# A decoder layer's expert stage: earlier statistics, a later weight request, token numbers from one accumulation

## The reference

```
x = x + self_attention(layernorm(x))                     # 16 heads, causal
x = x + cross_attention(layernorm(x), context, mask)     # 16 heads
x = x + experts(layernorm(x))

def experts(x):                       # x: 4096 tokens x 512
    probs = softmax(x @ Wg + bg)      # 8 experts
    a = argmax(probs)                 # one expert a token
    h = gelu(x @ W1[a] + b1[a])       # 512 -> 512
    y = h @ W2[a] + b2[a]             # 512 -> 512
    return probs[a] * y
```

## Time and profile before

| | us |
|---|---|
| median of 3 runs | 2126.4 (2125.07 to 2128.78) |
| the profiled execution | 2124.88 |
| its span, first to last instruction | 2123.1 |
| start of the expert stage | 1740.8 |
| first gather starts | 1810.8 |
| first tile's rows normalized from | 1820.7 |
| first tile's W1 matmuls from | 1825.0 |

### The profile page before, as it was taken

One profiled execution on the slowest core, in us unless ns is written; L12 is line 12 of the kernel. 1 busy time (PEld: TensorE's weight loads), 2 busy tenths in 40 slices (PEclk: granted clock), 3 DMA queues, 4 the chain that ended last, 5 costly groups with the idle time before them and its releaser, 6 DMA issues. The chain is left out here.

```text
span 2123.1 us, 34283 instructions
## 1 busy us (share of the span) xinstructions
PE 1914.8 (90%) x10910; PEld 1328.5 (63%) x10910; DVE 1384.7 (65%) x2824; ACT 1140.5 (54%) x2168; POOL 1006.4 (47%) x1030
## 2 busy tenths in 40 slices
PE   4899999999999856999999999999999965799997
PEld 3666666767676634556666666666566424698896
DVE  4666666666666625667767676767676527588886
ACT  3555555555555423555555555555555425587785
POOL 2446565564655652444444444344444326345544
PEclk9999999999999977999999999999999867799999
DMA  5334444444434334333434343434333239322220
GB/s 157 89 93 113 121 131 108 127 105 125 135 98 118 101 107 137 83 89 79 115 81 120 80 120 76 124 72 106 94 100 76 61 94 378 109 95 70 88 88 25
DMA packets 133301, 227.47 MB, mean 107 GB/s; under 512 B 30522, under 2 KB 31586, under 8 KB 133152
## 3 DMA queue, kind: packets, MB, share of 16 engines
q1 hardware_dynamic: 109920, 194.93, 33.2%
q0 software_dynamic: 12704, 29.51, 5.1%
q10 hardware_dynamic: 10528, 1.17, 0.4%
HBM read 94.92 MB, written 37.31 MB: 62 GB/s over the span
## 5 line engine op out<-in xcount | busy, mean ns | idle before, releaser
L391 POOL TENSOR_TENSOR cross_probs<-cross_probs 128x1024 f32<-128x1024 f32 x128 | 304.7, 2384 | 361.8 <-ACT cross_probs L493 361.1
L591 DVE TENSOR_REDUCE cross_m_col<-cross_sS 128x1 f32<-128x512 f32 x512 | 340.1, 686 | 186.4 <-PE cross_sS L744 182.7
L493 ACT ACTIVATE cross_probs<-cross_sT 128x512 f32<-128x512 f32 x512 | 305.5, 599 | 271.0 <-PE cross_sT L760 266.5
L594 DVE CUSTOM_DVE_ANT_0 self_sS<-self_sS,self_tri 128x128 f32<-128x128 f32 (+3 forms) x512 | 248.8, 503 | 184.5 <-PE self_sS L744 181.3
L493 ACT ACTIVATE self_probs<-self_sT 128x256 f32<-128x256 f32 (+3 forms) x512 | 222.7, 439 | 241.8 <-PE self_sT L760 238.9
L379 POOL TENSOR_SCALAR_AFFINE_SELECT self_probs<-self_probs 128x256 f32<-128x256 f32 x256 | 106.8, 423 | 324.0 <-ACT self_probs L493 324.0
L744 PE MATMUL cross_sS<-cross_stack 97*128 97x512 f32 x512 | 210.8, 420 | 29.1 <-DVE cross_m_col L591 19.0
L760 PE MATMUL cross_sT<-cross_stack 98*128 98x512 f32 x512 | 214.9, 433 | 2.2 <-ACT cross_probs L493 2.2
L391 POOL TENSOR_TENSOR self_probs<-self_probs 128x512 f32<-128x512 f32 (+1 forms) x128 | 210.9, 1668 | 0.3 <-ACT self_probs L493 0.3
L760 PE MATMUL self_sT<-self_stack 98*128 98x256 f32 (+2 forms) x512 | 176.1, 357 | 2.4 <-ACT self_probs L493 2.4
L760 PEld LDWEIGHTS cross_sT<-cross_stack 98*128 98x128 f32 x512 | 95.5, 192 | 130.4 <-ACT cross_probs L493 79.1
(11 more groups left out here) (244 smaller groups left out, 4600.1 us busy)
## 6 DMA issues: line engine op xcount, KB each, us to landing
self_stack<-self_stage SPq DMA_DIRECT2D x384, 128.0 KB, 2.4
cross_stack<-cross_stage SPq DMA_DIRECT2D x288, 128.0 KB
self_rows<-in_x_dram SPq DMA_DIRECT2D x64, 256.0 KB, 3.6
moe_w<-in_L_ffn_W_dram SPq DMA_DIRECT2D x16, 1024.0 KB, 14.8
cross_stack<-cross_stage POOLq DMA_DIRECT2D x96, 128.0 KB, 3.3
x_after_self<-self_rows SPq DMA_DIRECT2D x32, 256.0 KB, 2.4
x_after_self_and_bias<-self_ahead SPq DMA_DIRECT2D x32, 256.0 KB, 2.3
cross_rows<-x_after_self SPq DMA_DIRECT2D x32, 256.0 KB, 4.3
```

The source lines that it names most:

```text
L391: pool.tensor_tensor(total, total, tile_of(n, kb)[:, js, q0:S], ALU.add).then_inc(added, 1)
L493: act.activation(tile_of(n, kb)[:, j, q0:S], sT[:, i % 2, q0:S], ACT.Exp, scale=SCALE).then_inc(exp_done, 1)
L591: dve.tensor_reduce(to, sS[:, k % 2], AX_X, ALU.max).then_inc(s_free, 1)
L594: dve.tensor_tensor_reduce(sS[:, k % 2, 0:width], sS[:, k % 2, 0:width], tri[:, S - P - qb * P:S - P - qb * P + width], 1.0, LOWEST, ALU.a ...
```

## The change

- VectorE's and TensorE's waits for the constants move: VectorE's behind the statistics of batch 4, TensorE's (with b1's transpose) behind the first two turned tiles. ScalarE's copy of b1 goes behind the third turned tile.
- SyncE requests b2 for the first three tiles, then waits until the first tile's rows have been gathered, and only then requests expert 3's weights.
- The tile numbers carry 128 x tile - 8192 from the start (`iota`). So the products for partition and tile can be summed in one PSUM accumulation: 64 matmuls of 52 columns in place of 32 of 104. One VectorE step, done once for `cur` (6 columns) and once for `ids` (52), takes the place of three; the first three tiles' `cur` needs no copy on GpSimd.
- `weigh` of pairs 0 to 2 moves ahead of the last `choose`; the exponentials of pairs 0 to 2 move ahead of the last `take_gate`. Of the four stores only two stand ahead of ScalarE's part of `at_col`, the other two behind it. Gelu's table is loaded behind the stores.

```diff
-            for e in [e for e in range(E) if e != LENT] + [LENT]:
-                if e < NB:
+            for e in range(E):
+                if e < LENT:
                     sp.wait_ge(loaded[weight_sem[e]], 16)
-                if e == LENT:
-                    sp.wait_ge(placed, 4)
-                load_weights(e)
+                if e != LENT:
+                    load_weights(e)
             sp.wait_ge(experts_ready, 1)
...
+            for i in range(RING):
+                tile(0, i)
+            sp.wait_ge(placed, 4)
+            sp.wait_ge(loaded[weight_sem[LENT]], 16)
+            sp.wait_ge(gathered[0], 16 * R)
+            load_weights(LENT)
+            with sp.Fori(1, LAPS) as lap:
...
-            for n, step, base, of_p in ((NT, 1, -NO_ROW // P, 0), (1, 1, 0, 1), (LEVELS, TOK, 0, 0),
+            for n, step, base, of_p in ((NT, P, -NO_ROW, 0), (1, 1, 0, 1), (LEVELS, TOK, 0, 0),
...
+            def gather(t, i, copied=True):
+                if copied:
+                    pool.tensor_copy(cur[:, i], ids[:, bass.ds(t * R, R)]).then_inc(cur_ready, 1)
...
             for t in range(RING):
-                gather(t, t)
+                gather(t, t, copied=False)
+            pool.wait_ge(ids_ready, 2)
...
             normalize_batch(0)
-            act.wait_ge(const_step, 12)
-            act.wait_ge(g_full, 1)
-            act.copy(b1_cols[:].rearrange("p e k -> p (e k)"), b1_bank)
...
                 take_turned(b, 2)
+                if b == 0:
+                    act.copy(b1_cols[:].rearrange("p e k -> p (e k)"), b1_bank)
                 take_turned(b, 3)
+            for i in range(PAIRS - 1):
+                exponent(i)
             take_gate(B - 1)
-            for i in range(PAIRS):
-                exponent(i)
-            act.preload_act_table(ACT.Gelu)
-            for i in range(PAIRS):
+            exponent(PAIRS - 1)
+            for i in range(2):
                 store_rec(i)
...
                 act.activation(at_col[:, ts, 0], same_col[:, ts], ACT.Copy, scale=numbers_p).then_inc(col_ready[0], 1)
+            for i in range(2, PAIRS):
+                store_rec(i)
+            act.preload_act_table(ACT.Gelu)
...
-            dve.wait_ge(const_loaded, 16 * 3)
             for b in range(B):
                 row_stats(b)
+                if b == 4:
+                    dve.wait_ge(const_loaded, 16 * 3)
...
-            for i in range(2, PAIRS):
-                choose(i)
-                if i == 2:
-                    spread_counts(0)
+            choose(2)
+            spread_counts(0)
+            for i in range(PAIRS - 1):
+                weigh(i)
+            choose(PAIRS - 1)
             spread_counts(1)
-            for i in range(PAIRS):
-                weigh(i)
+            weigh(PAIRS - 1)
...
             dve.wait_ge(placed, 4)
-            step(dve.tensor_scalar(id_f, sorted_[:, 1], float(P), None, ALU.mult))
-            stepped()
-            step(dve.tensor_tensor(id_f, id_f, sorted_[:, 0], ALU.add))
-            stepped()
-            dve.tensor_scalar(ids[:], id_f, float(NO_ROW), None, ALU.add).then_inc(ids_ready, 1)
+            for to in (cur[:].rearrange("p i r -> p (i r)"), ids[:]):
+                n = to.shape[1]
+                dve.tensor_scalar(to, sorted_[:, 0:n], float(NO_ROW), None, ALU.add).then_inc(ids_ready, 1)
...
-            pe.wait_ge(const_loaded, 16 * 3)
-            pe.transpose(b1_bank, b1_rows, ident[0:E * KT, 0:E * KT])
             for b in range(B):
                 turn(b, 0)
                 turn(b, 1)
+                if b == 0:
+                    pe.wait_ge(const_loaded, 16 * 3)
+                    pe.transpose(b1_bank, b1_rows, ident[0:E * KT, 0:E * KT])
...
-                op = pe.matmul(sorted_.rearrange("p v c -> p (v c)"), at_row[:, t], at_col[:, t].rearrange("p v c -> p (v c)"),
-                               start=t == 0, stop=t == NT - 1)
+                for v in range(2):
+                    op = pe.matmul(sorted_, at_row[:, t], at_col[:, t, v], start=t == 0 and v == 0, stop=t == NT - 1 and v == 1)
```

More of the change, by code:

```diff
@@ L907, in expert_layer @@
         mv = take(2 * NB * 2).rearrange("p (a t s) -> p a t s", a=2, t=NB)
-        id_f = take(COLS)
         def table(n):
@@ L937, in expert_layer @@
         totals = [hidden[:, n, 0:1] for n in (1, 3)]
-        sorted_ = py[:, 0, 0:2 * COLS].rearrange("p (v c) -> p v c", v=2)
+        sorted_ = py[:, 0, 0:COLS]
         const_step, const_loaded = sem("const_step"), sem("const_loaded")
@@ L998, in tile @@
                 sp.dma_start(b2_rows[:, i], b2[bass.ds(e, 1)].rearrange("o d -> (o d)").partition_broadcast(P)).then_inc(b2_loaded[i], 16)
-            with sp.Fori(0, LAPS) as lap:
+            for i in range(RING):
[5 more added lines that the diff above has]
+            with sp.Fori(1, LAPS) as lap:
                 for i in range(RING):
@@ L1069, in _ @@
             pool.wait_ge(ids_ready, 1)
[L1071 to L1074, removed]
+            def gather(t, i, copied=True):
+                if copied:
+                    pool.tensor_copy(cur[:, i], ids[:, bass.ds(t * R, R)]).then_inc(cur_ready, 1)
+                    pool.wait_ge(cur_ready, t + (1 - RING))
+                    pool.sem_inc(waited, 1)
                 for r in range(R):
```

## The result

Over all runs measured for the first comparison the changed kernel took 2117.3 us (five runs, 2114.8 to 2123.2) against 2126.4 of before (by now five runs too): ratio 0.9962, 95% interval 0.9947 to 0.9978, faster by 4.7 to 11.3 us. Two later comparisons of the same two kernels gave 0.9972 (0.9960 to 0.9985) and 0.9974 (0.9960 to 0.9988), so 5.5 to 6.0 us is the better figure, and the 9.1 between the first medians was partly luck.

What follows compares the result with a forecast made beforehand. The front's chain of waits, not TensorE, was taken as what could be shortened. An earlier first gather (2.4 us) and its faster landing (4.6) sum to 7.0, taking the median 2126.4 to 2119.4 us; range 2115.5 to 2123.5.

Steps and rivals of the forecast that it cites:

- rival A: The forecast itself: the last store's landing at 1807.5 sets the first gather; 2119.4 us, bounds 2118.3 to 2121.5, chance 0.50.
- rival B: Stores don't bind; VectorE's sorted numbers set the first gather, at 1805.6, gain 9.8, so 2116.6 us; chance 0.22.
- Statistics: VectorE's first statistics start 4.5 us sooner, on x instead of the constants; net gain 4.35 at the last gate result.
- weigh: Three weighs moved ahead of the last `choose` on the same path lose between 0 and 1.0 us; 0.3 taken.
- Sorting matmuls: `at_row` becomes the bound; the last 16 matmuls take 1.35 us plus 0.3 to the result; numbers at 1804.7.
- The stores bind: GpSimd waits for all four stores, the last landing at 1807.5; first gather at 1808.4 against 1810.82, gain 2.4 us.
- The gather: Without expert 3's weights beside it, the first tile's second gather lands in 3.69 us, not 8.28; gain 4.6.
- b2's loads mostly lie in the shadow: b2's loads ahead of the gather, 0.75 MB or 2 us, are mostly hidden behind the wait for the stores.
- Sum: 2.4 us from the first gather's earlier start plus 4.6 from its faster landing make 7.0 us off the whole.
- C: The gather stays slow, as first of its kind or beside b2's loads; only 2.4 us gained, 2124.0; chance 0.14.
- D: The front's early start doesn't arrive; numbers at 1809.0, first gather at 1809.9, gain 5.5 us, 2120.9; chance 0.09.
- E: The late-issued stores keep their slow rate and land at 1816.5; first gather at 1817.4, 2128.4 us, slower; chance 0.05.

Runs made afterwards that it cites:

- run 5: Changed kernel with all four stores ahead of ScalarE's part of `at_col` again; ratio to the kernel before 0.9964 (0.9950 to 0.9978).
- run 4: Changed kernel with VectorE's wait for the three constants back ahead of the first statistics; ratio to the kernel before 0.9985 (0.9972 to 0.9998).
- run 6: Changed kernel with the weights of experts 5 to 7 also requested only behind the first tile's gather; ratio to the kernel before 0.9975 (0.9962 to 0.9988).
- Run 7: Changed kernel with b2's first three loads behind the first tile's gather, ahead of expert 3's weights; two ratios to the kernel before, 0.9959 and 0.9946.
- run 3: Changed kernel with expert 3's weights requested early again, ahead of b2 and the gathers; ratio to the kernel before 0.9986 (0.9975 to 0.9997).

## Why the prediction was right, point by point

The profile shows the mechanism of the forecast, rival A. The time by itself doesn't: 2117.3 lies in the whole range, but 2.1 below the 2119.4 forecast, outside A's own bounds (2118.3 to 2121.5) and nearer to rival B's 2116.6. That is the scatter of the first five runs. By the two later comparisons, 5.5 to 6.0 us below 2126.4, the time would be 2120.4 to 2120.9, 1.0 to 1.5 above the forecast and within A's bounds.

- **Statistics.** 4.5 us sooner at VectorE, GpSimd's second batch sooner by the same (15.44 of stage time against 19.93), and 4.49 left at the last gate copy in the first profile, 3.8 and 4.0 in the other two (forecast 4.35). The 0.15 for b1's copy is too small to be read in that.
- **weigh.** From the last gate copy to VectorE's step behind the placed counts it took 4.3 us in before (1790.55 to 1794.85) and 4.5 after (1790.33 to 1794.86): 0.23 lost, against 0.3.
- **Sorting matmuls.** `at_row` is the bound, as said. The term of the last 16 matmuls was mis-sized: from `at_row`'s end to VectorE's next step it took 1.0 us, 0.88 of it the matmuls, and not 1.35 + 0.3, since the pitch went down with the columns, from 84 to 44 ns. The numbers came 0.2 to 0.9 sooner than forecast (63.0, 63.7 and 63.4, forecast 63.9). The 107 ns a load that the Trainium skill's page gives ("TensorE: Matmul & The Clock Gate", "LDWEIGHTS (loading the stationary operand)") are over twice what these rows leave room for. It changed nothing, for the stores came later.
- **The stores bind.** The step that mattered. Forecast 66.7 of stage time, measured 66.3, 66.7 and 65.7; first gather 67.6, measured 67.2, 67.6 and 66.6. Runs 4 to 6 show the reason: with the fourth store asked for 1.8 to 2.5 us sooner (run 5) the landing doesn't move, with it asked for 4.3 to 5.0 later (run 4) it moves by 0.3 to 1.3, and without the weights beside it (run 6) it comes 6.4 to 7.4 us sooner.
- **The gather.** This term was too large: 3.7 us to land forecast, 4.9, 3.9 and 4.6 measured, so the gain is 3.4 to 4.4 and not 4.6. The step that failed is "b2's loads mostly lie in the shadow". They were asked for at 64.0 to 66.5 of stage time, landed 4.9 to 5.8 us after that in the first profile (3.3 to 4.2 in the other two), and so stood beside the gather, where the prediction had them done in 2 us. Run 7 shows it: with them behind, 3.5 us.
- **Sum.** 7.0 forecast at W1; 6.3, 6.8 and 7.1 measured in stage time, 6.0 to 8.3 at the end. The first medians' 9.1 holds some us of the attention layers. Two small slips in the prediction change nothing: its note of 4.35 + 0.5 + 0.5 gained ahead of the numbers doesn't match its own times, which give 4.5 there (1809.2 to 1804.7) and 5.2 ahead of the gather; and the range's lower end, 2115.5, lies 0.5 below B's early end by B's own rows (first gather at 1805.0, so 2116.0).
- **Rivals.** B (the numbers bind) did not occur, but holding expert 7 brings it about. C was partly true, through b2. D did not occur either; run 4 brings its front about and confirms its first gather (69.0, forecast 69.1), but not its sum: W1 came at 80.8 and not at 78.7, since the second gather was slow there. E's slow drain did not occur: the stores landed within about 4 us of the weights' end, at 65.7 to 66.7, not at E's 75.7.

What stays open: the part of the new order of `weigh` and the exponentials was read from the timeline and not tried alone; nor were the single accumulation and the direct write of `cur`. The two parts that were undone one at a time were worth 2.7 to 3.6 (run 3) and 3.0 to 3.8 us (run 4) at W1, of 6.3 to 7.1 in all. If parts may be added, little is left for the others: as long as the stores bind, what the numbers gain is lost in waiting.

## What to carry to other kernels

When a wait is removed, work out the landing times of everything that the next stage waits for, and ask which of them depend on bytes already queued and not on your engines: here 5.3 us gained in the front were 2.8 at its end. Small transfers on the critical path should not stand beside a bulk load that isn't due; hold back as much of the bulk as buys them a quiet DMA, but no more than is through again when the next latency-bound transfer starts (one expert here, not two, by one profile each). Where the rest of the program scatters by more than the change is worth, measure the stage from its own start.

## What was not expected of the hardware

- Issuing a store can block ScalarE: with the DMA full, the third and fourth of these stores (1024 pieces of 16 bytes each) took 3.3 and 6.0 us to issue in before, and none took over 0.60 us with the DMA free.
- The attention layers' time scatters by up to 6 us at the start of the cross layer between executions of the same code: its first product with V came between 861.6 and 867.8 us in seven profiles. Busy time by stretch, columns as above, of before and of the changed kernel (700 to 870 us from the start):

```profile
700.00:760.00 60.00, 49.61 (x294) 29.50 (x292) 29.24 (x85) 27.40 (x61) 37.66 (x42) 0.91 0.36 100
760.00:870.00 110.00, 67.59 (x279) 47.89 (x276) 47.28 (x65) 30.25 (x43) 36.56 (x41) 0.77 0.41 123
```

```profile
700.00:760.00 60.00, 52.12 (x281) 30.98 (x280) 28.24 (x83) 25.34 (x55) 34.17 (x39) 0.82 0.35 99
760.00:870.00 110.00, 66.63 (x269) 47.08 (x270) 46.21 (x62) 30.84 (x45) 37.10 (x43) 0.75 0.40 122
```

The granted clock of TensorE was 0.91 and 0.77 in the one, 0.82 and 0.75 in the other, and the first product with V of the cross layer came at 861.6 and 864.9. In these two the clock and the lateness go together, but not in all: the latest of the seven, 867.8 (expert 7's weights held), had 0.88. The cause stays open.
